# Products that nobody reads, put into TensorE's order of a two-layer transformer kernel

## The chip, the cores and the metric

One core of one Trainium2 chip runs the whole kernel. The metric is the device time of one execution in microseconds (us), the median of several runs; smaller is better.

## The reference, cut to what matters

The input is a batch of 8 sequences of 512 tokens by 256 features, in fp32. Four blocks follow one another, each wrapped the same way; what matters here is which matrix products there are.

```python
x = x + layernorm(attention0(layernorm(x)))   # 16 heads of 16, rope, causal softmax, biases
x = x + layernorm(gated_ffn0(layernorm(x)))   # silu(x Wg) * (x Wu), 768 wide, then Wd
x = x + layernorm(attention1(layernorm(x)))   # 16 heads of 64, 50*tanh(s/50), causal softmax
x = x + layernorm(token_shift_ffn(layernorm(x)))  # r = sigmoid(xr Wr); out = r * (relu(xk Wk)^2 Wv)
```

The attention of layer 0 has 16 heads of only 16 features; that of layer 1 has 16 heads of 64. Both mask with a lower triangle of 512 by 512.

## The kernel before, in words

**Precision.** Every weight and every activation that goes into a large product is split into a high and a low part (fp32r), and a product is three products: high by high, low by high, high by low (`split_terms`, L205; `product`, L336). The usual instruction on TensorE is therefore a product of 128 rows with 512 (or 256) columns.

**Two phases.** `phase1` (L356) does attention 0 and the gated ffn for all 8 batches, `phase2` (L1034) attention 1 and the token-shift ffn. The first writes its result to `x_mid` in DRAM, the second reads it.

**Pieces, rounds and the tables.** The work of a batch is cut into pieces ("rope", "max", "score", "pv", "o", "gate", ...). A table (L422 for layer 0, L1090 for layer 1) gives each piece a time. A round has 24 units of such time (`SLOTS`, L194). `Schedule` (L67) takes the quotient of a piece's time by 24 as the number of rounds by which it lags its batch, and the remainder as its place in the round. Every engine issues its own pieces in order of place; so the numbers only make an order for each engine, and semaphores do all the waiting. In one round of layer 0 TensorE works on the attention of batch b+1, on the ffn of batch b and on the projections of batch b+2. The middle rounds are a loop in the program; the first rounds and the last are written out. `start` (L499) merges the loading of weights (`loading_table`, L482) into the first round. `program` of phase 2 (L1190) merges layer 0's last rounds (`closing_table`, L1156), the loading of layer 1's weights (`prologue_table`, L1146) and layer 1's first rounds by `offset` (L1155).

**TensorE's pieces in layer 0.** "max" (`row_max`, L903) makes scores from 48 rows (L913) and adds a mask in bf16 (L920), for VectorE to take the row maxima (L782). "score" (L932) makes the scores again from 49 rows (L944), for ScalarE's exponential (L720). "pv" (L949) multiplies probabilities and values in four column strips of the array (L958). "outT", "att_T" and "x1_T" are transposes (L967, L978), "maxT" too (L928). "rope", "v", "o", "gate", "up" and "down" go through L340.

**The middle of a round.** After "o" of batch b VectorE has to form its statistics, its norm, the residual sum, the next statistics and the next norm (`o_out` to `x1_norm`, L811 to L837) before TensorE can transpose the result ("x1_T") and begin "gate". Meanwhile TensorE has only "max" and "score" of batch b+1, then "pv" of its first heads.

**Buffers in PSUM.** Rings of units (`Units`, L102) hold the results: `ring_d` for "max", "rope", "pv"; `ring_s` (two banks) for "score" and "v"; `ring_e` (banks 6 and 7) for "att_T", "o", "x1_T", "gate", "up", "down". `claim` (L162) makes TensorE wait until the unit's last user has been read. In phase 2 `ring_s` has two units of two banks for "v", "qk", "score", "x3_T", "r", "key" and "out".

**The end.** After the last attention piece "o" of batch 7 only "x3_T", "r", "key" and "out" are left for TensorE, and each waits for a chain over VectorE, ScalarE and GpSimd.

Of the kernel before, what the change touches and what calls it, by code (L numbers as in the profile page):

```python
# [27 lines left out]
P = 128  # L28
# [170 lines left out]
PLACED = 16 * 3 * 2  # L199
VSTEP = HD0 + 1  # L200
# [155 lines left out]
def phase1(nc, block, ctx, memory, a, x_mid, tok, banks, psum, ident, expo):  # L356
# [56 lines left out]
    with nc.sbuf_tensor("l0_staging", [P, 2 * NM, T], F32, side="right") as raw:  # L413
# [9 lines left out]
        "load_x": {(): -22.66},  # L423
        "x_stats": {(): -19.43},
        "x_rstd": {(): -21.11},
        "x_norm": {(): -18.09},
        "x_T": {(0,): -12.64, (1,): -12.6},
        "x_T_hi": {(0,): -13.41, (1,): -11.44},
        "x_T_lo": {(0,): -13.57, (1,): -13.43},
        "rope": {(0,): -6.98, (1,): -6.78, (2,): -0.17, (3,): 5.18},  # L430
# [1242 lines left out]
```

How the kernel before makes its waits and increments, by code:

```python
    def filled(self, eng, b, *use):  # L146
        eng.wait_ge(self.full, self.count(self.iteration(b, use), use, self.order))
# [1 line left out]
    def freed(self, eng, b, *use):  # L149
        eng.wait_ge(self.empty[self.freers[use]], self.count(self.iteration(b, use), use, self.group(use)))
# [11 lines left out]
    def claim(self, pe, b, *use, also=()):  # L162
        found = [user for user in (self.last_user(b, one) for one in (use, *also)) if user]
        for freer in self.empty:
            users = [user for user in found if self.freers[user[2]] == freer]
            if users:
                _, it, last = max(users, key=lambda user: user[0])
                pe.wait_ge(self.empty[freer], self.count(it, last, self.group(last)))
# [84 lines left out]
    def load(self, sp, n):  # L254
        if n >= self.slots:
            sp.wait_ge(self.low_done, n - self.slots + 1)
        sp.dma_start(self.raw(n), self.plan[n][0]).then_inc(self.loaded[n % self.slots], 16)
# [1 line left out]
    def high(self, act, n):  # L259
        act.wait_ge(self.loaded[n % self.slots], 16 * (n // self.slots + 1))
        self.nc.scalar.activation(self.plan[n][1], self.raw(n), ACT.Copy).then_inc(self.high_done, 1)
# [1 line left out]
    def low(self, dve, n):  # L263
        dve.wait_ge(self.high_done, n + 1)
        self.nc.vector.tensor_tensor(self.plan[n][2], self.raw(n), self.plan[n][1].bitcast(F32),
                                     ALU.subtract).then_inc(self.low_done, 1)
# [25 lines left out]
    def split(self, pe, i, count):  # L292
        if isinstance(i, int) and i == 0:
            pe.wait_ge(self.low_done, count)
```

## Time and profile before

| | |
|---|---|
| median of 3 runs | 1667.13 us (1666.17 to 1668.99) |
| profiled execution | 1666.39 us |
| its span, first to last instruction | 1664.6 us |
| TensorE busy | 1517.2 us, 91% of the span |
| VectorE, ScalarE, GpSimd busy | 1068.6, 833.4, 834.3 us |
| mean granted TensorE clock | 0.946 of 2.4 GHz |

The profile is of one execution. The span leaves out 1.8 us that lie around the first and the last instruction. In its views PE is TensorE, DVE VectorE, ACT ScalarE, POOL GpSimd, SP the queue that issues most DMAs. The granted clock is given as a share of 2.4 GHz: 1.00 is 2.4 GHz and 0.50 is 1.2 GHz; a value between them is a stretch that had both. "Busy" counts an engine as busy while an instruction of it is under way.

### The profile page before, as it was taken

How to read it: one execution, taken by the hardware profiler on the slowest of the kernel's cores; microseconds unless marked ns; L12 is line 12 of the kernel's file. 1: busy time of each engine (PE TensorE's matmuls, PEld its weight loads, DVE VectorE, ACT ScalarE, POOL GpSimd, SP SyncE). 2: the span in 40 equal slices, each digit the busy share in tenths (PEclk: the TensorE clock that was granted, in tenths of full speed). 3: DMA queues.
4: the chain of work that ended last, by engine and by line, in shares of the span. 5: the costliest groups of instructions: out<-in, count | busy, mean ns of one | idle time of the engine just before them, and what ended most of it. 6: DMA issues, size and time to landing. Idle time of an engine off the chain costs nothing.

```text
span 1664.6 us, 29499 instructions
## 1 busy us (share of the span) xinstructions
PE 1517.2 (91%) x11040; PEld 1090.6 (66%) x11040; DVE 1068.6 (64%) x1796; ACT 833.4 (50%) x1205; POOL 834.3 (50%) x1012
## 2 busy tenths in 40 slices
PE   3698999999998989898999999999999999999953
PEld 2455666757576766666767777777767677777742
DVE  4556676777767676666664667566675766666562
ACT  2233444443444435354465665756666566665621
POOL 2132433434344434343556666766658566585642
PEclk9677999999999999998999999999999999999986
DMA  6333333332323333321110001010000101000000
GB/s 145 68 52 52 52 64 52 52 56 36 61 37 61 42 63 40 64 90 39 45 39 1 1 5 35 1 39 1 27 10 0 38 0 38 0 1 26 1 26 13
DMA packets 46770, 61.34 MB, mean 37 GB/s; under 512 B 4928, under 2 KB 31968, under 8 KB 46688
## 3 DMA queue, kind: packets, MB, share of 16 engines
q1 hardware_dynamic: 45824, 59.56, 18.3%
q8 instruction: 55, 0.90, 0.2%
q10 hardware_dynamic: 864, 0.66, 0.1%
q14 instruction: 27, 0.22, 0.1%
HBM read 26.35 MB, written 8.39 MB: 21 GB/s over the span
## 4 chain that ended last, share of the span: by engine, by line
PE 83%; DVE 8%; ACT 3%; issue 2%; POOL 2%; DMA 2%; SPq 1%; POOLq 0%; DVEq 0%; ACTq 0%
PE psum L340 41%; PE psum L1588 8%; PE psum L1563 8%; PE psum L1604 5%; PE psum L958 5%; PE psum L1576 4%; PE psum L944 4%; PE psum L913 3%; DVE l_rowmax L782 2%; PE psum L920 1%; ACT l_probs L1369 1%; PE psum L978 1%; ACT l_probs L720 1%; PE psum L967 1%; PE psum L928 1%
## 5 line engine op out<-in xcount | busy, mean ns | idle before, releaser
L720 ACT ACTIVATE l_probs<-psum 128x512 f32<-128x512 f32 (+1 forms) x384 | 181.1, 524 | 243.9 <-PE psum L944 243.8
L1448 DVE RECIPROCAL l_att<-psum 128x512 f32<-128x512 f32 x64 | 214.8, 3356 | 96.5 <-PE psum L1576 86.3
L782 DVE TENSOR_REDUCE l_rowmax<-psum 128x2 f32<-128x1024 f32 (+3 forms) x256 | 200.8, 818 | 58.3 <-PE psum L920 57.6
L1369 ACT ACTIVATE l_probs<-psum 128x1024 f32<-128x1024 f32 (+1 forms) x192 | 163.8, 879 | 136.2 <-PE psum L1563 136.2
L221 POOL TENSOR_SCALAR_AFFINE_SELECT l_probs<-l_probs 128x256 f32<-128x256 f32 (+1 forms) x384 | 180.6, 502 | 0.0
L1439 DVE TENSOR_TENSOR l_qk_lo<-psum,l_qk_hi 128x1024 fp32r<-128x1024 f32 x64 | 77.9, 1218 | 143.2 <-ACT l_qk_hi L1359 143.2
L1375 ACT ACTIVATE l_probs<-l_probs 128x2048 f32<-128x2048 f32 (+1 forms) x128 | 160.1, 1270 | 1.3
L216 POOL TENSOR_TENSOR l_pool_holder<-expo 128x1 f32<-128x1 f32 x128 | 29.2, 228 | 243.3 <-ACT l_probs L720 121.8
L1588 PE MATMUL psum<-l_probs,l_v 128*64 128x512 f32 (+3 forms) x1024 | 150.7, 436 | 0.0
L1588 PEld LDWEIGHTS psum<-l_probs,l_v 128*64 128x64 f32 x1024 | 70.4, 137 | 83.3 <-issue 69.0
L1311 POOL TENSOR_TENSOR l_attT_lo<-l_att,l_attT_hi 128x512 fp32r<-128x512 f32 x64 | 93.7, 1469 | 61.4 <-ACT l_attT_hi L1387 61.2
L1303 POOL TENSOR_TENSOR l_keysum<-l_probs 128x768 f32<-128x768 f32 x64 | 118.2, 1846 | 6.9 <-POOL l_probs L221 0.4
L944 PE MATMUL psum<-l_qT,l_kT 49*128 49x512 f32 (+3 forms) x512 | 96.8, 415 | 25.7 <-ACT l_probs L720 23.5
L913 PE MATMUL psum<-l_kT,l_qT 48*128 48x512 f32 (+3 forms) x512 | 88.0, 384 | 27.7 <-DMA l_qT<-l_roped_hi 12.5
L667 POOL TENSOR_TENSOR l_hT_lo<-l_gated,l_hT_hi 128x512 fp32r<-128x512 f32 x48 | 61.8, 1287 | 90.0 <-ACT l_hT_hi L734 90.0
L650 POOL TENSOR_TENSOR l_roped_lo<-l_straight,l_turned 128x512 f32<-128x512 f32 x32 | 41.1, 1285 | 130.7 <-DVE l_turned L775 125.0
L1359 ACT ACTIVATE l_qk_hi<-psum 128x1024 fp32r<-128x1024 f32 x64 | 65.8, 1028 | 77.1 <-PE psum L340 77.1
L1563 PE MATMUL psum<-l_qk_hi 64*128 64x512 f32 (+3 forms) x512 | 96.9, 373 | 6.3 <-ACT l_probs L1369 2.8
L328 POOL TENSOR_TENSOR l_x_rstd<-l_x_veps,expo 128x4 f32<-128x4 f32 x48 | 50.8, 1058 | 98.4 <-DVE l_x_veps L322 97.8
L958 PE MATMUL psum<-l_probs,l_v 128*32 128x512 f32 (+3 forms) x1024 | 94.8, 521 | 0.0
L913 PEld LDWEIGHTS psum<-l_kT,l_qT 48*128 48x128 f32 x512 | 50.6, 207 | 54.2 <-issue 32.4
L1305 POOL TENSOR_TENSOR l_keysum<-l_keysum,l_probs 128x512 f32<-128x512 f32 x64 | 83.4, 1303 | 5.0
(196 smaller groups left out, 4173.9 us busy)
## 6 DMA issues: line engine op xcount, KB each, us to landing
l_kT<-l_roped_hi SPq DMA_DIRECT2D x64, 128.0 KB, 4.0
l_qT<-l_roped_hi SPq DMA_DIRECT2D x64, 128.0 KB, 5.8
l_xin<-in_x SPq DMA_DIRECT2D x8, 512.0 KB, 5.0
l_kT<-l_roped_lo SPq DMA_DIRECT2D x32, 128.0 KB, 5.1
l_qT<-l_roped_lo SPq DMA_DIRECT2D x32, 128.0 KB, 6.4
l_x<-in_x SPq DMA_DIRECT2D x8, 512.0 KB, 4.0
x_mid<-l_x SPq DMA_DIRECT2D x8, 512.0 KB, 4.6
l_xin<-x_mid SPq DMA_DIRECT2D x8, 512.0 KB, 4.4
```

What stands on the lines that cost most here:

```text
L221: nc.gpsimd.affine_select(out=part, in_=part, compare_op=ALU.is_ge, fill=0.0, base=0, pattern=[[0, part.shape[1]], [1, P]], channel_multip ...
L340: last = nc.tensor.matmul(out, l(c), r(c), start=(k == 0), stop=(k == len(todo) - 1))
L720: ring_s.free(nc.scalar.activation(probs[:, SLOT[p], e, c0:c1], ring_s.unit(*use)[:, 0:c1 - c0], ACT.Exp, scale=HD0 ** -0.5), *use)
L782: reduced = nc.vector.tensor_reduce(rowmax[:, t, a // 2, :, a % 2], ring_d.unit("max", a, k)[:, :, c0:c0 + (t + 1) * P], mybir.AxisListTyp ...
L913: nc.tensor.matmul(unit[:, e, c0:c0 + (t + 1) * P], qT[rows, a, t * P:(t + 1) * P], kT[rows, a, 0:(t + 1) * P], start=(c0 == 0), stop=False)
L944: last = nc.tensor.matmul(ring_s.unit("score", p, u, e)[:, c0:c0 + T - kt * P], kT[rows, p, kt * P:(kt + 1) * P], qT[rows, p, kt * P:T], s ...
L958: last = nc.tensor.matmul(ring_d.unit("pv", g)[32 * j:32 * j + 32, 0, kt * P:T], v0[:, kt, h * VSTEP:h * VSTEP + 32], probs[:, SLOT[p], j ...
L1369: ring_s.free(nc.scalar.activation(probs[:, p % 2, :, c0:c1], ring_s.unit("score", p, u)[:, :, 0:c1 - c0], ACT.Tanh, scale=HD1 ** -0.5 / C ...
L1375: nc.scalar.activation(part, part, ACT.Exp, scale=CLAMP).then_inc(exped.sem, 1)
L1448: ring_d.free(nc.vector.reciprocal(att[p % 2][:], ring_d.unit("den", p)), "den", p)
L1563: last = nc.tensor.matmul(ring_s.unit("score", p, u)[:, e, c0:c0 + T - kt * P], l[half, slot, 1, kt * P:(kt + 1) * P], r[half, slot, 0, kt ...
L1588: last = nc.tensor.matmul(ring_d.unit("pv", p)[64 * e:64 * e + 64, kt * P:T], v1[:, kt, 2 * p + e, :], probs[:, p % 2, e, OFF1[kt]:OFF1[kt ...
```

## The change

It adds matrix products whose results nobody reads. `heat` issues `count` products of 128 rows by 128 weights with 512 columns. They stand in three places:

- "warm": 16 pieces of 2 products in TensorE's order of layer 0's first round, into bank 7, which no piece uses in that round. They wait for nothing.
- "heat": 3 pieces of 2 products in each of layer 0's rounds for the 8 batches, at places 13.30, 14.90 and 15.28, that is after "o" and before "x1_T". They claim the unit of `ring_e` that "x1_T" will take. For batch 7 the closing table puts all three after layer 1's second "qk" piece.
- "end_heat": 9 pieces of 6 products, for batch 7 alone. They claim the unit of the piece that follows ("x3_T", "r" or "out"). In the last round the first stands after "o" of pair 3, the second after "o" of pair 5, the third between "o" of pair 7 and "x3_T"; three between "x3_T" and "r"; three between "key" and "out".

All other numbers of the tables change too, by amounts that swap neighbours in the engines' orders. No piece is added beside these, and none is removed.

```diff
+START_HEATS = 16
+ROUND_HEATS = 3
+END_HEATS = 9
...
+def heat(nc, out, w, count):
+
+    for _ in range(count):
+        nc.tensor.matmul(out, w[:, 0, 0:P], w[:, 0, 0:T], start=True, stop=True)
...
-        "score": {(0, 0): 9.1, (0, 1): 9.89, (0, 2): 11.93, (1, 0): 12.95, (1, 1): 14.48, (1, 2): 15.27, (2, 0): 15.31,
+        "score": {(0, 0): 8.67, (0, 1): 9.75, (0, 2): 12.12, (1, 0): 12.87, (1, 1): 14.74, (1, 2): 15.17, (2, 0): 15.37,
...
-        "x1_T": {(0,): 40.2, (1,): 40.82},
+        "x1_T": {(0,): 41.07, (1,): 41.07},
...
+        "heat": {(0,): 37.3, (1,): 38.9, (2,): 39.28},
...
+        "warm": {(0,): 1.4, (1,): 1.77, (2,): 2.92, (3,): 4.82, (4,): 5.99, (5,): 7.25, (6,): 7.8, (7,): 8.58, (8,): 9.46, (9,): 12.28, (10,): 12.35, (11,): 14.2, (12,): 15.5, (13,): 17.55, (14,): 18.78, (15,): 23.9},
...
+        def warm(n):
+
+            heat(nc, banks[7], wqk[0], 2)
+
+        def warm_round(i, n):
+
+            ring_e.claim(pe, i, "x1_T", 0)
+            heat(nc, ring_e.unit("x1_T", 0), wgu[0], 2)
...
+        "end_heat": {(0,): 26.17, (1,): 30.91, (2,): 38.43, (3,): 39.88, (4,): 41.31, (5,): 41.52, (6,): 42.61, (7,): 44.75, (8,): 44.97},
...
-    offset = 242.15
+    offset = 240.24
...
+        "heat": {(0, 7): 244.453, (1, 7): 244.505, (2, 7): 244.558},
...
+        def end_heat(i, n):
+
+            if isinstance(i, int) and i == BATCH - 1:
+                following = "x3_T" if n < 3 else "r" if n < 6 else "out"
+                ring_s.claim(pe, i, following)
+                heat(nc, ring_s.unit(following)[:, 0, :], wrkv[0], 6)
```

By the new tables TensorE's order in the middle of a layer-0 round becomes: "o" (second half), "score" (1,0), heat, "max" (4,0), "maxT", "score" (1,1), heat, "max" (4,1) and (4,2), "score" (1,2), heat, "score" (2,0), "max" (5,0), "pv" (0), "score" (2,1), "max" (5,1), "rope" (0), "x1_T". Before, "x1_T" (0) stood right behind "pv" (0), ahead of "score" (2,1), "max" (5,1) and "rope" (0), and its second half ahead of that "rope".

## Rows read from the trace of the kernel before

**Rows 1.** The page: busy time of the engines, and the chain that ended last.
```profile
PE 1517.2 (91%) x11040; PEld 1090.6 (66%) x11040; DVE 1068.6 (64%) x1796; ACT 833.4 (50%) x1205; POOL 834.3 (50%) x1012
...
PE 83%; DVE 8%; ACT 3%; issue 2%; POOL 2%; DMA 2%; SPq 1%; POOLq 0%; DVEq 0%; ACTq 0%
```

**Rows 2.** The page: granted clock in 40 slices of the span, in tenths.
```profile
PEclk9677999999999999998999999999999999999986
```

**Rows 3.** Windows, TensorE alone: stretch, length, busy us (instructions), granted clock, DMA.
```profile
45.00:127.00 82.00, 67.90 (x462) 0.67 0.33 55
136.00:144.00 8.00, 7.13 (x56) 0.57 0.26 51
157.00:168.00 11.00, 8.98 (x68) 0.53 0.01 1
249.00:257.00 8.00, 6.28 (x47) 0.57 0.01 3
...
693.00:701.00 8.00, 6.86 (x54) 0.57 0.01 2
754.00:766.00 12.00, 8.73 (x31) 0.57 0.44 131
```

**Rows 4.** Windows, TensorE alone: the long stretches of both layers, and the end.
```profile
180.00:740.00 560.00, 526.62 (x4272) 0.96 0.33 55
800.00:1590.00 790.00, 783.24 (x5408) 1.00 0.05 16
1590.00:1664.00 74.00, 28.98 (x165) 0.69 0.07 22
```

**Rows 5.** Timeline of TensorE, middle of a layer-0 round: start, us, line, gap before and its releaser.
```profile
426.13 0.38 PE L944 MATMUL psum<-l_qT,l_kT 49*128 49x256 f32 x2 [1.17 <-ACT l_probs L720]
427.26 0.80 PE L944 MATMUL psum<-l_qT,l_kT 49*128 49x512 f32 x2 [0.74 <-ACT l_probs L720]
...
429.28 0.79 PE L913 MATMUL psum<-l_kT,l_qT 48*128 48x512 f32 x2 [0.83 <-DVE l_rowmax L782]
...
430.19 4.16 PE L958 MATMUL psum<-l_probs,l_v 128*32 128x512 f32 x32
434.32 0.66 PE L978 MATMUL psum<-ident,l_gated 128*128 128x128 f32 x4
```

**Rows 6.** Windows, TensorE alone, around the same place of that round.
```profile
413.00:416.00 3.00, 2.64 (x24) 1.00 0.84 126
...
424.00:427.00 3.00, 1.21 (x18) 1.00 0.48 169
427.00:430.00 3.00, 1.92 (x12) 0.51 0.00 0
```

**Rows 7.** Timeline of TensorE: products at both levels of the clock.
```profile
749.25 2.36 PE L958 MATMUL psum<-l_probs,l_v 128*32 128x512 f32 x32
...
762.01 0.63 PE L340 MATMUL psum<-l_xT_hi,l_wq_lo 128*128 128x512 f32 x1
762.44 0.63 PE L340 MATMUL psum<-l_xT_hi,l_wq_hi 128*128 128x512 f32 x1
...
1639.08 0.39 PE L340 MATMUL psum<-l_mixk_hi,l_wrkv_hi 128*128 128x512 f32 x1
1639.31 0.39 PE L340 MATMUL psum<-l_mixk_lo,l_wrkv_hi 128*128 128x512 f32 x1
```

**Rows 8.** Windows, TensorE alone: the end of the kernel.
```profile
1604.00:1608.00 4.00, 0.56 (x5) 1.00 0.39 131
1608.00:1611.00 3.00, 2.55 (x12) 0.51 0.44 139
...
1624.00:1634.00 10.00, 0.00 (x0) 0.50 0.00 0
1634.00:1639.00 5.00, 4.96 (x24) 0.52 0.00 0
...
1642.00:1648.00 6.00, 0.03 (x1) 0.80 0.00 0
1648.00:1653.00 5.00, 5.00 (x24) 0.56 0.00 0
```

More of the change, by code:

```diff
@@ new lines, in phase1 @@
+        "x_T_hi": {(0,): -13.01, (1,): -11.01},
+        "x_T_lo": {(0,): -13.31, (1,): -12.99},
+        "rope": {(0,): -7.32, (1,): -6.78, (2,): -1.09, (3,): 5.18},
+        "roped": {(0,): -8.61, (1,): -5.33, (2,): 0.74, (3,): 4.84},
+        "rope_sum": {(0,): -10.57, (1,): -8.49, (2,): 2.44, (3,): 3.85},
+        "rope_hi": {(0,): -4.41, (1,): -3.91, (2,): 6.25, (3,): 6.5},
+        "rope_lo": {(0,): -6.33, (1,): -3.74, (2,): 6.23, (3,): 7.06},
+        "place": {(0,): -1.66, (1,): -1.47, (2,): 8.29, (3,): 8.95},
@@ new lines, in phase1 @@
+        "outT_norm": {(0,): 19.3, (1,): 26.21, (2,): 29.66, (3,): 31.89},
+        "att_T": {(0,): 34.01, (1,): 34.47},
+        "att_T_hi": {(0,): 34.59, (1,): 34.72},
+        "att_T_lo": {(0,): 33.16, (1,): 34.17},
+        "o": {(0,): 35.64, (1,): 36.15},
+        "o_out": {(0,): 34.45, (1,): 35.85},
+        "x1_T": {(0,): 41.07, (1,): 41.07},
+        "x1_T_hi": {(0,): 40.99, (1,): 41.13},
+        "x1_T_lo": {(0,): 39.99, (1,): 40.94},
+        "o_stats": {(): 36.13},
+        "o_rstd": {(): 34.77},
@@ new lines, in phase1 @@
+        "hidden": {(0,): 44.69, (1,): 48.09, (2,): 49.93, (3,): 51.31, (4,): 52.39, (5,): 53.02},
+        "hidden_hi": {(0,): 45.77, (1,): 47.6, (2,): 50.21, (3,): 50.43, (4,): 53.71, (5,): 54.94},
+        "hidden_lo": {(0,): 43.71, (1,): 45.49, (2,): 45.93, (3,): 50.21, (4,): 51.99, (5,): 51.99},
+        "down": {(0,): 55.87, (1,): 56.16, (2,): 56.2, (3,): 56.69},
+        "heat": {(0,): 37.3, (1,): 38.9, (2,): 39.28},
+        "x2_stats": {(): 55.56},
+        "x2_rstd": {(): 57.81},
+        "x2_norm": {(): 56.21},
@@ new lines, in phase2 @@
+        "x3_T_out": {(): 37.36},
+        "mix": {(0,): 39.34, (1,): 41.51},
+        "mix_hi": {(0,): 37.7, (1,): 40.28},
+        "mix_lo": {(0,): 38.18, (1,): 38.82},
+        "r": {(): 41.72},
+        "r_out": {(): 41.76},
+        "key": {(): 42.25},
+        "key_out": {(): 42.2},
+        "square": {(): 42.09},
+        "kact_hi": {(): 43.99},
+        "kact_lo": {(): 46.6},
+        "out": {(): 45.41},
+        "out_out": {(): 47.32},
+        "gate": {(): 47.36},
+        "x4_stats": {(): 47.9},
@@ new lines, in phase2 @@
+        "att_T": {(0, 7): 239.67, (1, 7): 241.68},
+        "o": {(0, 7): 243.927, (1, 7): 244.163},
+        "heat": {(0, 7): 244.453, (1, 7): 244.505, (2, 7): 244.558},
+        "x1_T": {(0, 7): 245.73, (1, 7): 245.94},
+        "gate": {(0, 7): 246.66, (1, 7): 247.28, (2, 7): 248.997, (3, 7): 249.06, (4, 7): 249.32, (5, 7): 250.287},
+        "up": {(0, 7): 246.83, (1, 7): 247.56, (2, 7): 249.003, (3, 7): 249.11, (4, 7): 249.48, (5, 7): 250.383},
+        "down": {(0, 7): 251.912, (1, 7): 252.094, (2, 7): 252.276, (3, 7): 252.458},
@@ L1631, in key @@
             ring_s.fill(last, "key")
[L1633 removed]
+        program(pe, {"end_heat": end_heat, "x_T": x_T, "v": v, "qk": projected, "score": score, "den": den, "pv": pv, "o": o,
                      "x3_T": x3_T, "key": key, "r": tokens("r", mixr, slice(0, D), mix_split, 2 * NC),
```

242 lines of the change are left out of this document (98 added, 144 removed).

## The prediction, made before the changed kernel ran

> **What bounds the kernel now.** I read the page first. TensorE is busy for 91% of the span and makes 83% of the chain that ended last [rows 1]. Its clock comes next, as it decides what a busy microsecond is worth: full nearly everywhere, but low at the start, at the end, and dented between them [rows 2]. The windows place the dents [rows 3]. In the first round TensorE is busy for 67.9 of 82 us at a mean clock of 0.67; then come a dip at 136, one in the middle of each of seven rounds (at 157, 249, 338, 427, 515, 604 and 693 us; the first, second and last are shown) and one where the layers meet, at 754. Layer 1 has none: 783.2 of 790 us busy at 1.00, so it can hardly gain [rows 4]. The end is the opposite: 29.0 us busy of 74, at 0.69.
>
> What a stretch would give at full clock I take as its busy time times what the clock lacks of 1.00 (work done in B us at a mean clock c fills B times c at full clock). It overrates where another engine's chain sets the pace, as the gaps stay. The sum: first round 67.9 x 0.33 = 22.4 us; dip at 136, 3.1; at 157, 4.2; six others between 2.7 and 3.0, together 17; at 754, 3.8; the end 29.0 x 0.31 = 9.0, of which 2.0 would only widen gaps, so 7. In all 57 us, 3.4% of the time: the most that a full clock could bring before its price.
>
> Why does it fall? In the round at 427 no gap is long: 1.17, 0.74 and 0.83 us, behind ScalarE's exponentials and VectorE's maxima [rows 5]. But from 424 to 427 TensorE was busy for only 1.21 of 3 us, with products of 48 and 49 rows, and the clock fell right after; where it was busy for 2.64 of 3 it stayed full [rows 6]. It came back only behind the "pv" group, which took 4.16 us there and 2.36 us at full clock [rows 5, 7].
>
> A page of the Trainium skill reads differently: "TensorE: Matmul & The Clock Gate", section "Why this matters for your kernels", asks for no long idle gaps between bursts and says nothing against many short ones. By it these dips should not be there; the trace disagrees, with 1.17 us the longest gap in front of the fall. What that would mean for the change is a rival below.
>
> **The change, part by part.** A product costs 0.23 us at full clock and 0.43 us at the low one, the distance of two starts [rows 7]. Its result goes to PSUM units that are free, so apart from TensorE's time it costs only its `claim`. No DMA is added, and SP's order swaps only weight fetches and one "maxima" with neighbours that wait for other things; I cost that at nothing, hidden behind TensorE.
>
> *First round, 32 products.* The first pair stands behind the first "max", whose DMA ends at about 45 us, so the clock is already low when it comes; nothing stands in the idle stretch ahead. I take 60% of the 22.4 us as regained, 13.4: the first pairs need some us to lift the clock, and two products every 3 to 5 us will not hold it each time. Bounds: 0% and 100%. Price: 32 x 0.23 = 7.4 us, and some 10 of them at the low level add 2.0. TensorE is idle for 14.1 us here; with 2.7 us of the products in such gaps, 6.7 stay on the path. Net 6.7 faster; bounds 13.7 slower (none regained, all 32 at 0.43 on the path) and 20 faster.
>
> *Layer-0 rounds, 6 products each.* The three pieces stand behind "score" (1,0), (1,1) and (1,2), where TensorE next waits for ScalarE: gaps of about 0.7, 1.17 and 0.74 us against 0.46 us a pair. So they cost nothing while those gaps last; without the cover, 6 x 0.23 = 1.4 us a round. The `claim` waits for VectorE's read of "o", done before. Seven rounds hold 4.2 + 17 = 21 us. I take three quarters, 15.9 us: the gap of 0.83 at 428 has no product in it, and "pv" could still meet a low clock. What is late next is VectorE's norm: "x1_T" waits for it at 434.3, and a "pv" faster by 1.8 us would meet that wait. The new order puts "rope" (12 to 24 products, 2.8 to 5.5 us) ahead of "x1_T", which covers it. Bounds: 21 faster; 7 x 1.4 = 9.8 slower.
>
> *Batch 7's six.* They come behind "qk", after the gaps that lower the clock at 754, so they don't lift it; two transposes for layer 1 move ahead of "att_T", into such a gap. Net 0.5 faster; bounds 1.4 slower, 3.8 faster.
>
> *The end, 54 products.* "x3_T" stays low: only 6 products precede it in more than 10 us of idleness. Between "x3_T" and "r" 18 run for 4.1 to 7.7 us of the 10 idle ones; "r" took 4.96 us at 0.52 and would take 2.7 [rows 8]. I count 1.3 of those 2.2, since some idle time is left before "r". Behind "key" 18 at full clock fill 4.1 of 6 us, and "out" (5.00 us at 0.56, so 2.2 to gain) gets 1.8. The 6 in front of "o" of pairs 6 and 7 lie in the gap at 1604 and give 0.6 of 1.2. Sum 3.7 faster; bounds 2 slower (a group late by its own length delays what is queued behind it), 6.3 faster. All of them finish, by the lengths above, before their follower is ready.
>
> *The other places.* They swap neighbours. Layer 1 has 6.8 us of idle time in all, so they can't gain there, and could lose; the retuned order of layer 0 could give or take a few us. I take 0, bounds 8 either way.
>
> Sum: 6.7 + 15.9 + 0.5 + 3.7 = 26.8 faster. Against the profiled execution, 1666.4 - 26.8 = 1639.6; that execution lies 0.7 us below the median shown, so I say 1640.
>
> **The rivals.**
>
> *Nearly all the clock comes back.* The places look fitted to the gaps, and the first round's pairs are spread over all of it. Then about 52 of 57 us return, less 9 of price: 1667 - 43 = 1624. Against it: the dip at 754 has no products ahead of it, and "x3_T" stays low. 0.15.
>
> *The rounds' dips stay.* Six short products do not outweigh 48-row work and gaps; or, as that page has it, only long gaps matter, and what fills short ones does nothing. Then the 15.9 are gone, and the first round nets about 3: 1667 - 7 = 1660. For it: between 427 and 430 TensorE was busy for 1.92 of 3 us even at half speed [rows 6]. Against it: 0.92 us of full-height products in a stretch busy for 1.21 of 3 is a large addition. 0.14.
>
> *The new order gives part of it back.* Layer 1 runs at 99% busy; 1.5 us lost in each of its 8 rounds make 12: 1652. 0.10.
>
> *Slower: the products queue in front of work that is ready.* TensorE takes them in order. If the clock stays low in the first round, 32 x 0.43 = 13.7, less 4 in gaps, are 10 us lost; in the rounds half of 8 x 6 x 0.23 lies on the path, 5.5; at the end 1: 1667 + 16 = 1683. It decides once less than a third of the first round's 22 us and none of the dips come back. 0.07.
>
> The same page, in its section on what happens when a matmul is issued, says that products stay in program order while only weight loads are pulled ahead. That is the rule against this change; no row here shows a product overtaking another, and by its figure for 512 columns back to back (about 0.22 us) the 32 would cost 6.9 us instead of 7.4.
>
> That the products are dropped is no case: they are plain instructions, and 134 of them (32 + 48 + 54) will be there.
>
> **How the numbers follow.** The forecast has 0.54, its own range 1630 to 1652; the rivals as given. The range holds all of the first, most of the second, the order's case and the nearer part of the dips' case: 1622 to 1660. Below it lies 0.07, above it 0.13. A measurement of this kernel can tell about 0.2% (3.3 us) from no change. Faster by more than that: 0.88. Within it: 0.04. Slower: 0.08.
>
> **What would show it.** First round: the mean clock of its window at 0.8 or more, and its length down by 5 to 9 us although 32 products are added. Rounds: no value below 1.00 around "pv" (0) in at least five of seven, "pv" at 2.4 us, the round 2 to 3 us shorter. End: "r" and "out" together down from 10 to about 7 us. Layer 1: the loop's rounds equal to within 0.5 us. I am wrong if the clock still falls in front of "pv" (0) in most rounds, if the mean clock of the first round stays under 0.75, or if ScalarE's or VectorE's waits in front of "score" and "max" grow by what the clock gave.

## The result: 1.2% slower, and the profile after

| | before | after |
|---|---|---|
| median of the runs made side by side | 1667.44 us (1666.17 to 1668.99, 4 runs) | 1689.32 us (1682.62 to 1689.98, 4 runs) |
| span of the profiled execution | 1664.6 us | 1687.1 us |
| mean granted TensorE clock | 0.946 | 0.965 |

The ratio is 1.0122, 95% interval [1.0095, 1.0149]. The forecast was 1640 us, and its range ended at 1660: wrong by sign. The clock rose as meant, and the time rose too.

The page of the changed kernel: busy time, granted clock in 40 slices, shares of the chain that ended last. It answers to [rows 1, 2].

```profile
PE 1540.6 (91%) x11174; PEld 1110.6 (66%) x11174; DVE 1085.9 (64%) x1796; ACT 825.3 (49%) x1205; POOL 823.2 (49%) x1012
...
PEclk9789999999999999999999999999999999999997
...
PE 75%; DVE 7%; issue 5%; ACT 5%; POOL 3%; DMA 3%; SPq 2%; POOLq 0%; ACTq 0%; DVEq 0%
```

TensorE held 83% of the chain before and holds 75% now; ScalarE, POOL, DMA, SP's queue and "issue" have gained shares. So other engines end more waits. The waits of TensorE name one (line, releaser: us in all, times, longest):

```profile
PE psum L924 <- DMA l_qT<-l_roped_hi: 26.8, 6, 14.6
```

Before, this wait came once, with the 12.5 us of the first round. Now it comes five times more, 12.2 us together: "max" waits for the load of the q rows. Windows of TensorE in the changed kernel (stretch, length, busy us, clock, DMA share, GB/s), against [rows 3, 4, 8]:

```profile
45.00:127.00 82.00, 66.59 (x474) 0.79 0.40 59
...
153.00:242.00 89.00, 83.14 (x688) 1.00 0.34 50
...
331.00:423.00 92.00, 85.93 (x688) 0.96 0.31 52
...
474.00:478.00 4.00, 4.00 (x18) 0.57 0.20 69
...
1657.00:1661.00 4.00, 4.00 (x19) 0.50 0.00 0
```

The first stretch's clock went from 0.67 to 0.79. Two rounds (from 153 and from 242) have no dip at all. From 331 on the old dip is back, and a second one stands 50 us into the round (474 to 478), behind the new wait. "r" at the end (1657) is as slow as before. Both are in the timeline of the round that begins at 423.6, "pv" (0) and "max" (0,0):

```profile
436.61 4.05 PE L969 MATMUL psum<-l_probs,l_v 128*32 128x512 f32 x32 [0.18 <-DVE l_rowmax L793]
...
473.96 0.50 PE L924 MATMUL psum<-l_kT,l_qT 48*128 48x512 f32 x2 [1.92 <-DMA l_qT<-l_roped_hi]
```

To say where time went I cut each trace where "x_T" starts: at the third round, at the last round of layer 0's loop, at layer 1's second round, at its last. Lengths in us of all kernels of this study, from their profiled executions:

| kernel | to the third round | layer-0 rounds | join of the layers | layer-1 rounds | end |
|---|---|---|---|---|---|
| before | 149.7 | 444.6 | 269.7 | 612.7 | 187.9 |
| after | 153.1 | 454.6 | 274.3 | 613.7 | 191.4 |
| tables_only | 154.7 | 462.6 | 272.5 | 613.6 | 191.0 |
| products_only | 151.0 | 451.1 | 269.0 | 612.7 | 186.2 |
| pool_order | 152.3 | 454.3 | 273.1 | 613.7 | 190.9 |
| pool_swap_alone | 146.3 | 485.1 | 284.8 | 612.8 | 189.2 |
| rope_chain | 148.3 | 438.3 | 268.7 | 613.7 | 190.9 |
| rope_pool | 149.4 | 438.2 | 270.0 | 613.8 | 192.4 |
| old_layer0 | 150.9 | 449.9 | 268.5 | 613.7 | 191.4 |
| mask_alone | 148.7 | 455.1 | 273.8 | 613.7 | 192.4 |
| mask_early | 152.3 | 470.3 | 274.8 | 612.5 | 187.9 |
| repaired_bare | 147.6 | 443.3 | 272.6 | 613.7 | 191.3 |
| round_only | 149.9 | 445.6 | 269.0 | 612.7 | 187.9 |
| end_only | 144.9 | 447.7 | 269.0 | 612.5 | 184.2 |
| warm_only | 151.8 | 447.5 | 272.4 | 612.7 | 188.7 |
| warm_early | 148.9 | 447.6 | 272.5 | 612.6 | 188.8 |
| round_double | 149.5 | 448.7 | 270.2 | 612.7 | 186.8 |
| chain_double | 151.3 | 434.4 | 270.7 | 613.7 | 191.3 |
| x1_behind | 150.2 | 460.3 | 274.6 | 612.7 | 187.8 |
| x1_behind_end | 148.8 | 463.2 | 276.3 | 612.7 | 186.6 |

The 22.5 us of the change are 3.4 + 10.0 + 4.6 + 1.0 + 3.5. A row is one execution: that of `rope_chain` was its fastest (1661.6 us, median 1666.0), the others lie nearer to their medians.

### The profile page after: what moved, and what is told of

Same layout as the page of the kernel before. It is cut to its first block, busy times and chain, and to the rows that moved or that the text cites. A ratio compares the mean times of both kernels' runs of the same rounds, so it can differ in the third digit from the quotient of the medians.

```text
span 1687.1 us, 29762 instructions
## 1 busy us (share of the span) xinstructions
PE 1540.6 (91%) x11174; PEld 1110.6 (66%) x11174; DVE 1085.9 (64%) x1796; ACT 825.3 (49%) x1205; POOL 823.2 (49%) x1012
## 4 chain that ended last, share of the span: by engine, by line
PE 75%; DVE 7%; issue 5%; ACT 5%; POOL 3%; DMA 3%; SPq 2%; POOLq 0%; ACTq 0%; DVEq 0%
PE psum L343 37%; PE psum L1611 8%; PE psum L1586 7%; PE psum L1627 5%; PE psum L969 4%; PE psum L1599 4%; PE psum L955 3%; PE psum L924 3%; ACT l_probs L1392 2%; DMA l_qT<-l_roped_hi 2%; DVE l_rowmax L793 2%; SPq L603 1%; ACT l_probs L731 1%; PE psum L931 1%; PE psum L989 1%
## 5 line engine op out<-in xcount | busy, mean ns | idle before, releaser
L224 POOL TENSOR_SCALAR_AFFINE_SELECT l_probs<-l_probs 128x256 f32<-128x256 f32 (+1 forms) x384 | 174.3, 486 | 0.0
L924 PE MATMUL psum<-l_kT,l_qT 48*128 48x512 f32 (+3 forms) x512 | 84.6, 368 | 45.0 <-DMA l_qT<-l_roped_hi 26.8
L1334 POOL TENSOR_TENSOR l_attT_lo<-l_att,l_attT_hi 128x512 fp32r<-128x512 f32 x64 | 85.8, 1340 | 36.8 <-ACT l_attT_hi L1410 36.7
L924 PEld LDWEIGHTS psum<-l_kT,l_qT 48*128 48x128 f32 x512 | 48.0, 196 | 74.0 <-issue 39.2
L661 POOL TENSOR_TENSOR l_roped_lo<-l_straight,l_turned 128x512 f32<-128x512 f32 x32 | 41.2, 1287 | 96.0 <-DVE l_turned L786 88.5
L969 PE MATMUL psum<-l_probs,l_v 128*32 128x512 f32 (+3 forms) x1024 | 86.0, 482 | 2.0 <-POOL l_probs L224 1.2
```

The source lines that it names most:

```text
L224: nc.gpsimd.affine_select(out=part, in_=part, compare_op=ALU.is_ge, fill=0.0, base=0, pattern=[[0, part.shape[1]], [1, P]], channel_multip ...
L924: nc.tensor.matmul(unit[:, e, c0:c0 + (t + 1) * P], qT[rows, a, t * P:(t + 1) * P], kT[rows, a, 0:(t + 1) * P], start=(c0 == 0), stop=False)
L969: last = nc.tensor.matmul(ring_d.unit("pv", g)[32 * j:32 * j + 32, 0, kt * P:T], v0[:, kt, h * VSTEP:h * VSTEP + 32], probs[:, SLOT[p], j ...
```

## The experiments

**1. Order or products?** `tables_only` is the changed kernel without its 134 products, `products_only` the kernel before with them. `pool_order` takes one swap on POOL back in the changed kernel. `pool_swap_alone` moves one place in the kernel before; by its number "hidden_lo" (0) passes not only "rope_lo" (1) but "mask" (3) too, which it does not pass in the changed kernel.

```diff
 tables_only, against after: the lines "warm", "heat", "heat" (closing) and "end_heat" removed
 products_only, against before: these lines added; "end_heat": {(0,): 28.7, (1,): 30.91, (2,): 37.0,
   (3,): 38.5, (4,): 40.0, (5,): 41.0, (6,): 42.61, (7,): 44.0, (8,): 44.9}, "heat" of batch 7 at 246.2 to 246.4
 pool_order, against after
-        "rope_lo": {..., (1,): -3.74, ...
+        "rope_lo": {..., (1,): -4.5, ...
 pool_swap_alone, against before
-        "hidden_lo": {(0,): 44.58, ...
+        "hidden_lo": {(0,): 42.9, ...
```

> The changed kernel without any of its 134 extra products; all other new places stay. Theory O (the new order costs, the products are about neutral): about 1680 us, at least 1675. Theory P (the products queue in front of ready work, the order is neutral): 1663 to 1670 us, like the kernel before.

> The kernel before with the same three kinds of extra products (32 + 48 + 54), at the same places in TensorE's order as far as the old order has them (the nine at the end stand at the end's gaps, the first of them behind the last score of pair 7). Theory O: 1655 to 1668 us, no slower than before. Theory P: 1680 us or more.

> The changed kernel with one swap undone on GpSimd: the low part of the second rope piece goes ahead of the low part of the first hidden piece again, in every layer-0 round. If that swap makes TensorE wait 1.9 us for the placed rows of q in front of the first max and lets the clock fall a second time in a round (worth 1.7 us), as the trace of after suggests, about 3.5 us come back in each of 5 or 6 rounds: 1668 to 1674 us. If the swap is not the cause (theory P, or another swap): 1686 us or more.

> The kernel before with that one swap made on GpSimd and nothing else. If it is a cause by itself: 8 to 20 us slower than before (1675 to 1687), with a wait for the rows of q in each round. If it needs the other new places: within 3 us of before.

Measured, against before: `tables_only` 1695.3 us, 1.0170 [1.0153, 1.0187]; `products_only` 1671.6 us, 1.0033 [1.0021, 1.0045]; `pool_order` 1687.4 us, 1.0126 [1.0109, 1.0143]; `pool_swap_alone` 1719.5 us, 1.0312 [1.0295, 1.0329].

The other places alone cost more than the whole change. The products alone cost 5 us on before's places and give 6 on the new ones (1695.3 to 1689.3). Both runs on POOL missed what was expected of them. The single swap back gave 2 us instead of 15 to 20. One number moved on POOL cost 52 us instead of 8 to 20, and by another wait than the changed kernel has, in TensorE's "pv" for POOL's masks:

```profile
PE psum L958 <- POOL l_probs L221: 36.0, 7, 5.4
```

The wait for the q rows stayed there as it was before (13.2 us in all, before 12.5), and in the changed kernel "pv" waits for a mask once, for 1.2 us. So POOL's order matters, but `pool_swap_alone` is no copy of the changed kernel's fault. POOL in a steady round of the kernel before (start, us, line, operation, gap before and its releaser); L650 forms a rotary sum, L654 its low part ("rope_lo"), L221 masks:

```profile
440.86 1.29 POOL L650 TENSOR_TENSOR l_roped_lo<-l_straight,l_turned 128x512 f32<-128x512 f32 x1 [8.01 <-DVE l_turned L775]
...
444.97 1.28 POOL L654 TENSOR_TENSOR l_roped_lo<-l_roped_lo,l_roped_hi 128x512 fp32r<-128x512 f32 x1 [1.36 <-ACT l_roped_hi L698]
446.21 1.29 POOL L650 TENSOR_TENSOR l_roped_lo<-l_straight,l_turned 128x512 f32<-128x512 f32 x1
450.13 1.28 POOL L654 TENSOR_TENSOR l_roped_lo<-l_roped_lo,l_roped_hi 128x512 fp32r<-128x512 f32 x1 [2.63 <-ACT l_roped_hi L698]
```

And the same in the changed kernel, whose lines are L661, L665 and L224:

```profile
446.17 1.29 POOL L661 TENSOR_TENSOR l_roped_lo<-l_straight,l_turned 128x512 f32<-128x512 f32 x1 [6.76 <-DVE l_turned L786]
...
450.30 1.28 POOL L661 TENSOR_TENSOR l_roped_lo<-l_straight,l_turned 128x512 f32<-128x512 f32 x1 [1.39 <-DVE l_turned L786]
456.03 0.19 POOL L219 TENSOR_TENSOR l_pool_holder<-expo 128x1 f32<-128x1 f32 x1 [4.45 <-ACT l_probs L731]
456.17 1.36 POOL L224 TENSOR_SCALAR_AFFINE_SELECT l_probs<-l_probs 128x512 f32<-128x512 f32 x3
457.49 1.29 POOL L665 TENSOR_TENSOR l_roped_lo<-l_roped_lo,l_roped_hi 128x512 fp32r<-128x512 f32 x1
```

Before, the first low part comes 4.1 us after its sum. After, "mask" (3) stands between (place 16.89 instead of 20.52, with "rope_lo" (0) at 17.67): POOL waits 4.45 us for ScalarE's exponential, and the low part comes 11.3 us after its sum. Behind it hang the copies of the k rows ("place" (0), after "rope_lo" (0)) and of the q rows ("place" (1), after "rope_lo" (1)), and behind these "max" (0,0).

**2. Repairs of the changed tables.** `rope_pool` moves two places on POOL, `mask_alone` only the second of them, `rope_chain` one on ScalarE as well; `old_layer0` takes layer 0's places from before.

```diff
 rope_pool, against after (mask_alone: the "mask" line alone)
-        "rope_lo": {..., (1,): -3.74, ...
+        "rope_lo": {..., (1,): -4.5, ...
-        "mask": {..., (3,): 16.89, ...
+        "mask": {..., (3,): 19.6, ...
 rope_chain: this, and
-        "rope_hi": {(0,): -4.41, ...
+        "rope_hi": {(0,): -5.9, ...
 old_layer0: layer 0's table and the loading table of before, with the lines "warm" and "heat"
```

> As rope_chain, but only the two places on POOL are moved (rope_lo 1 and mask 3); ACT keeps the changed kernel's order, rope_hi (0) behind maxT_out (2) and tanh (0). It tells POOL's part from ACT's. If POOL's mask (3), which waits 4.45 us for exp (3,2) in front of rope_lo, is the whole cause: equal to rope_chain within 3 us. If ACT's rope_hi is late by itself: within 3 us of the changed kernel (1684 to 1690), and only rope_chain is faster. Theory P: no effect, 1684 to 1690.

> The changed kernel (1689 us) with three places of layer 0's table moved, so that the rotary pieces of the next batch come first on their engines: rope_lo (1) and mask (3) on POOL (order rope_lo 0, rope_lo 1, mask 3, hidden_lo 0), and rope_hi (0) on ACT from -4.41 to -5.9, ahead of exp (3,1) and maxT_out (2). The 134 products and all else stay. Theory O (the tables' other places cost the time, through the late placing of q and k rows: max (0,0) waits for the l_qT load, TensorE idles and its clock falls a second time): the wait of L924 for l_qT shrinks from 26.8 us to under 14, the second dip of the steady rounds goes, a steady round takes 88.5 to 90 us instead of 92.0, the total 1667 to 1676. Theory P (products queued in front of ready work cost the time; the load's wait is a by-product): 1684 to 1690. Theory R (one place repaired only passes the wait on to the next one, as with rope_lo alone, which gave 2 us): the l_qT wait shrinks but max or rowmax waits grow as much, 1680 to 1688.

> The changed kernel with one place moved: layer 0's mask (3) on POOL from 16.89 to 19.6, behind rope_lo (0) and ahead of hidden_lo (0); rope_lo (1) stays at -3.74, behind hidden_lo (0). rope_lo (1) alone gave 2 us (1687.4), both together 24 us (1665.3). If mask (3) in front of rope_lo (0) is the whole cause (POOL waits 4.45 us for exp (3,2) there): 1665 to 1670. If the two only work together (rope_lo (1) behind hidden_lo (0) is late by itself, and either one delays the q rows): 1680 to 1688. If each takes its share: 1670 to 1680.

> The changed kernel with layer 0's table and the loading table as before, plus the 32 + 18 + 30 products of the first round and the rounds; layer 1's table, the prologue, offset and closing tables and the 54 end products stay those of the change. It splits the cost of the new places by layer. If the cost sits in layer 0's steady rounds (3.5 us in each of six) and layer 1 costs 0.65 us in each of seven rounds, 2 at the join and 3 to 5 at the end: 1677 to 1682. If layer 0 holds all of it: 1670 to 1674 (as the products on the old places, 1671.6). If layer 1 and the join hold most: 1684 or more.

Measured: `rope_pool` 1665.3 us, 0.9997 [0.9985, 1.0009]; `rope_chain` 1666.0 us, 0.9992 [0.9977, 1.0008]; `mask_alone` 1690.0 us, 1.0138 [1.0105, 1.0170]; `old_layer0` 1677.0 us, 1.0064 [1.0040, 1.0087].

Two numbers of the tables, both of POOL's pieces, take 24 us away by the medians, 21 by the two ratios (1.0122 and 0.9997). ScalarE's place adds nothing. TensorE's wait in `rope_pool`:

```profile
PE psum L924 <- DMA l_qT<-l_roped_hi: 15.9, 2, 14.6
```

Each number alone gives nothing (`pool_order` 2 us, `mask_alone` none). In `mask_alone` the mask is out of the way, but "rope_lo" (1) still stands behind "hidden_lo" (0) of the gated ffn, which waits for ScalarE in its turn:

```profile
451.03 1.27 POOL L665 TENSOR_TENSOR l_roped_lo<-l_roped_lo,l_roped_hi 128x512 fp32r<-128x512 f32 x1 [3.30 <-ACT l_roped_hi L709]
...
458.87 1.28 POOL L678 TENSOR_TENSOR l_hT_lo<-l_gated,l_hT_hi 128x512 fp32r<-128x512 f32 x1 [5.11 <-ACT l_hT_hi L745]
```

"max" needs the rows of both. SP's queue shows why each fault alone is enough. The copies it issues for "place" (0), k, and "place" (1), q, in `after`, in `pool_order` and in `rope_pool`:

```profile
458.86 2.55 SPq L603 DMA_DIRECT2D l_kT<-l_roped_hi  x4
465.27 1.18 SPq L603 DMA_DIRECT2D l_qT<-l_roped_hi  x2
```

```profile
457.71 2.56 SPq L603 DMA_DIRECT2D l_kT<-l_roped_hi  x4
461.68 1.19 SPq L603 DMA_DIRECT2D l_qT<-l_roped_hi  x2
```

```profile
444.83 2.56 SPq L603 DMA_DIRECT2D l_kT<-l_roped_hi  x4
448.81 1.18 SPq L603 DMA_DIRECT2D l_qT<-l_roped_hi  x2
```

The rounds begin at 423.6, 422.5 and 412.3 us. In these traces the twelve copies of a round land about 1.06 us apart. With only "rope_lo" (1) mended the q copies are issued 2.5 us earlier (39.2 us into the round, not 41.7), but they queue behind the k copies, which still start at 35.2, and the last lands at 50.1 us (50.2 in the changed kernel). In `mask_alone` the k copies start at 32.5, but the q copies only at 41.6, and the last lands at 50.0. With both mended it lands at 47.4 (before: 46.8), and "max" no longer waits. So two faults that each hold the same piece look like none when only one is mended. In `old_layer0` layer 1's rounds and end are as long as in the changed kernel (613.7 and 191.4 us, before 612.7 and 187.9), so layer 1's new places cost about 4.5 us. Which of them do was not tried.

**3. The mirror.** `mask_early` moves the mask alone in the kernel before. There it passes not only both "rope_lo" but also the second sum, "rope_sum" (1), which stays ahead of it in the changed kernel.

```diff
-        "mask": {(0,): 12.65, (1,): 13.31, (2,): 15.86, (3,): 20.52, ...
+        "mask": {(0,): 12.65, (1,): 13.31, (2,): 15.86, (3,): 15.865, ...
```

> The mirror: the kernel before, without any product, with one place moved, mask (3) on POOL from 20.52 to 15.865, ahead of rope_lo (0). If that order costs what the tables cost: a steady round of 91 to 92.5 us instead of 88.6, a new wait of L923's line for the l_qT load, a second clock dip beside the first, and a total of 1682 to 1696. If it is the combination with the change's other places that costs (in the tables of before rope_hi (0) stands earlier on ACT, so that rope_lo has slack): 1666 to 1672.

Measured: 1697.95 us, 1.0182 [1.0161, 1.0203]; a steady round takes 94.2 us. Both are above what was expected (1682 to 1696, 91 to 92.5), and the path is another one. Its POOL:

```profile
465.96 0.19 POOL L216 TENSOR_TENSOR l_pool_holder<-expo 128x1 f32<-128x1 f32 x1 [6.02 <-ACT l_probs L720]
466.10 1.35 POOL L221 TENSOR_SCALAR_AFFINE_SELECT l_probs<-l_probs 128x512 f32<-128x512 f32 x3
467.42 1.29 POOL L654 TENSOR_TENSOR l_roped_lo<-l_roped_lo,l_roped_hi 128x512 fp32r<-128x512 f32 x1
468.67 1.26 POOL L650 TENSOR_TENSOR l_roped_lo<-l_straight,l_turned 128x512 f32<-128x512 f32 x1
```

and two of its waits, of ScalarE and of TensorE:

```profile
ACT l_roped_hi L698 <- POOL l_roped_lo L650: 44.0, 10, 8.5
...
PE psum L944 <- ACT l_probs L720: 43.6, 32, 4.0
```

Here the second sum is late too (468.67), ScalarE stands 44.0 us in all in front of its "rope_hi" (15.3 before) with exponentials queued behind, and TensorE waits 43.6 us for these (23.5 before) instead of for the load. So a mask too early costs here too, but this is not the changed kernel's path; that one is shown by the repairs, where only the two numbers differ.

The Trainium skill, "PSUM — Partial Sum Buffer", section "Engine vs sequencer instructions", calls the queues of ScalarE, VectorE and GpSimd strictly first in, first out. The trace agrees: in the changed kernel ScalarE had finished the high parts by 455.3 us, and yet POOL began the low part at 457.49, behind the mask for which it had sat idle for 4.45 us.

**4. The products without the fault.** `repaired_bare` is `rope_chain` without any of the 134 products.

> rope_chain (1666.0 us) without its 134 products: the changed tables with the rotary pieces in front. It gives what the products are worth on an order that does not wait for l_qT. On the tables of before they cost 4.8 us (1671.6 against 1666.8), on those of the change they gave 6 (1689.3 against 1695.3). If they only fill a hole that the late rows made: 1658 to 1664. If they hold the clock whatever the order: 1669 to 1675. In the steady rounds I expect 2.9 us of clock lost instead of 1.7 or none, against 2.2 us of work less: 88 us a round, no change.

Measured: 1671.8 us, 1.0034 [1.0023, 1.0046]. So the products give about 6 us on the repaired order (1666.0 against 1671.8). The total is that of the second case, in which they hold the clock whatever the order. It is not so everywhere: they gain in layer 0 (the loop's rounds 443.3 to 438.3 us, the join 272.6 to 268.7 by the fastest execution, 270.0 by that of `rope_pool`), nothing at the end, and on before's places they cost.

**5. One kind of product at a time,** on before's places: `round_only` (48), `end_only` (54), `warm_only` (32).

> The kernel before with the 48 products of layer 0's rounds alone (six a round in front of pv 0); no start or end products, no other place moved. My prediction gave 15.9 us for this. From products_only (a steady round 88.6 us with and without them: 1.3 us of clock and 1.0 us of gaps filled against 2.2 us of added work) it should be neutral: 1664 to 1669. If the products in front of the late dip really were worth three quarters of the 21 us and the start products ate it: 1648 to 1656. If they only queue in front: 1672 to 1678.

> The kernel before with the 54 end products alone (places 28.7 to 44.9 of layer 1, last batch). My prediction gave 3.7 us for them; products_only's end stretch was 1.6 us shorter than before's. If the forecast's mechanism holds at that size: 1664 to 1666, r and out at 2.7 to 4 us instead of 5.0. If they only queue: 1667 to 1669.

> The kernel before with the 32 start products alone, at the change's places 1.4 to 23.9 of the first round. My prediction gave 6.7 us net for them. Of the 4.8 us that all products cost on the tables of before (1671.6), the rounds' own cost 3.3 (1670.1) and the end's gave 5 (1661.6), so that about 5 to 7 are left for the start products: 1669 to 1674, with the first x_T of batch 2 at 151 us instead of 149.7 and the next at 245 instead of 239.6. If the prediction's mechanism held: 1658 to 1662.

Measured: `round_only` 1670.1 us, 1.0018 [1.0004, 1.0032]; `end_only` 1661.6 us, 0.9970 [0.9953, 0.9986]; `warm_only` 1677.2 us, 1.0066 [1.0054, 1.0079]. Their sum is 9 us slower (3.0 - 5.0 + 11.0), all three together 5.5. Each lies outside what was expected of it: `round_only` by 1 us and `warm_only` by 3 on the slow side, `end_only` by 2 on the fast side.

The end pays: 5.0 us (2.3 to 7.8 by the interval), 3.7 were forecast. TensorE in `end_only` (the 18 products, and the start of "r" and of "out"):

```profile
1621.06 6.63 PE L350 MATMUL psum<-l_wrkv_hi 128*128 128x512 f32 x18 [1.11 <-ACT l_xs L1420]
1630.38 0.36 PE L343 MATMUL psum<-l_wrkv_hi,l_mixr_hi 128*128 128x256 f32 x1 [2.69 <-POOL l_mixk_lo L1336]
...
1636.07 4.27 PE L350 MATMUL psum<-l_wrkv_hi 128*128 128x512 f32 x18
1642.21 0.36 PE L343 MATMUL psum<-l_wrkv_hi,l_kact_hi 128*128 128x256 f32 x1 [1.88 <-POOL l_kact_lo L1341]
```

"r" runs at full clock here (a window from 1630.3 to 1633.1 shows 1.00; before, 0.52 [rows 8]), "out" only at its start. The end stretch is 3.7 us shorter, as large as the sum's term. Another execution shows less: with the same products in the same places "r" takes 4.5 us in `products_only` and 4.6 in `x1_behind_end`, not the 3.0 of this one, and their end stretches are 1.7 and 1.3 us shorter than before's; that of `round_double`, which has no product there, is 1.1 shorter.

**6. The first round: place or price?** `warm_early` puts all 16 pairs ahead of "max" (0,0), into the 12.5 us of its wait.

```diff
+        "warm": {(0,): 0.05, (1,): 0.095, ... (15,): 0.725},   (in steps of 0.045)
```

> As warm_only, but all 16 pairs stand ahead of max (0,0) (places 0.05 to 0.73), in the 12.5 us in which TensorE waits for the first l_qT load (32.5 to 45.0 us). 32 products take 7.4 us at full clock and 13.8 at the low one, so they fit or nearly. If the place is what was wrong (the clock is low when the first pair comes): the clock is full from 45 us on for at least a few us, the first batch is 2 to 5 us shorter, 1662 to 1666. If the sparse work behind it lets the clock fall again whatever stands ahead: no gain, 1665 to 1669, and the window 45 to 82 us at the same mean clock as before (0.67) within 0.07. If they delay the loads or the first max: 1670 or more.

Measured: 1672.8 us, 1.0039 [1.0026, 1.0051]. Timeline and windows of TensorE:

```profile
32.02 7.42 PE L350 MATMUL psum<-l_wqk_hi 128*128 128x512 f32 x32
44.69 0.80 PE L923 MATMUL psum<-l_kT,l_qT 48*128 48x512 f32 x2 [5.25 <-issue]
```

```profile
32.00:45.00 13.00, 7.75 (x35) 0.96 1.09 138
45.00:52.00 7.00, 5.80 (x46) 0.50 0.11 33
45.00:82.00 37.00, 26.70 (x180) 0.64 0.39 60
```

The 32 run at full clock and delay nothing ("max" starts at 44.69 us; 44.99 before). But 5.25 us of idle time follow, and the window from 45 to 52 us stands at 0.50, that from 45 to 82 at 0.64, as before. The case of "no gain whatever stands ahead" holds for this stretch (72.5 us against 73.0); the total was above it, by 4 us, for time lost further on (below, at the first round's step).

**7. Twice as many products.** `round_double` is `round_only` with 12 products a round, `chain_double` is `rope_chain` with 12.

```diff
-            heat(nc, ring_e.unit("x1_T", 0), wgu[0], 2)
+            heat(nc, ring_e.unit("x1_T", 0), wgu[0], 4)
```

> round_only (1670.1 us) with twice as many products: four for each heat piece, so 12 a round, 96 in all. Tells whether the rounds' term fails for want of products or by their price. Price in full: 48 x 0.23 = 11 us more, less what falls into gaps. If six were too few to hold the clock and twelve hold it: the dip in front of pv (0) goes (1.6 us a round) for 1.4 us of price, 1669 to 1673. If the dip does not come from those gaps alone: 1676 to 1682, a steady round 90 us instead of 88.6.

> rope_chain (1666.0 us: the changed kernel with its rotary pieces in front) with four products for each heat piece, 12 a round. There two kinds of steady rounds stand: 88.3 us with a dip worth 1.7 in front of pv (0), and 87.0 us without. If twelve hold the clock in every round and the added work lies in TensorE's wait for VectorE's maximum (1.45 us idle at 12.2 us of the round): rounds of 87.0 us, 1658 to 1663. If the added work lies on the path: 1668 to 1674.

Measured: `round_double` 1671.1 us, 1.0033 [1.0016, 1.0050]; `chain_double` 1662.7 us, 0.9974 [0.9965, 0.9984]. What a steady round of layer 0 is made of (the clock's loss is busy time times what the clock lacks of 1.00, summed over windows of half a microsecond; work is busy time less that loss):

| kernel, products a round | length | idle | loss | work |
|---|---|---|---|---|
| before, 0 | 88.6 | 4.9 | 2.9 | 80.8 |
| round_only, 6 | 88.6 | 4.0 | 1.6 | 83.0 |
| round_double, 12, from 421 | 88.6 | 4.3 | 0.0 | 84.3 |
| repaired_bare, 0 | 88.8 | 6.0 | 2.5 | 80.3 |
| rope_chain, 6, most rounds | 88.3 | 4.1 | 1.7 | 82.5 |
| rope_chain, 6, round at 411 | 87.0 | 4.1 | 0.0 | 82.9 |
| chain_double, 12, all | 87.0 | 2.8 | 0.0 | 84.2 |
| tables_only, 0 | 92.2 | 7.8 | 4.2 | 80.3 |
| after, 6, from 331 | 92.0 | 6.0 | 3.4 | 82.6 |

Twelve hold the clock in every steady round on the repaired order, and in the last two (from 421 and 510) on before's places. There it changes nothing: 88.6 us three times. The timelines tell why. `round_only` and `round_double`, "pv" (0) and then "x1_T":

```profile
431.55 3.54 PE L968 MATMUL psum<-l_probs,l_v 128*32 128x512 f32 x32
435.68 0.66 PE L988 MATMUL psum<-ident,l_gated 128*128 128x128 f32 x4 [0.58 <-DVE l_gated L335]
```

```profile
434.11 2.36 PE L968 MATMUL psum<-l_probs,l_v 128*32 128x512 f32 x32 [0.18 <-DVE l_rowmax L792]
438.37 0.66 PE L988 MATMUL psum<-ident,l_gated 128*128 128x128 f32 x4 [1.90 <-DVE l_gated L335]
```

From the start of their rounds (417.0 before, 418.3, 421.0) "x1_T" begins at 17.3, 17.4 and 17.4 us. "pv" got faster by 1.8 us (4.16 in [rows 5], 2.36 here), and the wait for VectorE's norm grew to 1.90 us. In the changed order "rope" (0) stands between "pv" and "x1_T", and no such wait is left. `chain_double`:

```profile
424.06 0.50 PE L924 MATMUL psum<-l_kT,l_qT 48*128 48x512 f32 x2 [0.23 <-DVE l_rowmax L793]
424.84 2.36 PE L969 MATMUL psum<-l_probs,l_v 128*32 128x512 f32 x32 [0.18 <-DVE l_rowmax L793]
431.22 0.82 PE L989 MATMUL psum<-ident,l_gated 128*128 128x128 f32 x6
```

Here the gain reaches the round: 87.0 us. The six further products filled what was a wait of 1.45 us for VectorE's maxima in `rope_chain`, and cost nothing.

**8. Taking that wait away on before's places.** `x1_behind` is `round_only` with "x1_T" behind "rope" (0); `x1_behind_end` adds the end products and has 12 a round.

```diff
-        "x1_T": {(0,): 40.2, (1,): 40.82},
+        "x1_T": {(0,): 41.07, (1,): 41.1},
```

> round_only (1670.1 us: the kernel before with the 48 round products) with x1_T moved behind rope (0) in TensorE's order (40.2 and 40.82 to 41.07 and 41.1), as in the changed table. In all three of before, round_only and round_double x1_T starts 17.4 us after the round's x_T, held by VectorE's norm (idle 0.4, 0.9, 2.3 us), and a steady round takes 88.6 us whatever the clock does; in the changed tables rope (0) stands between and covers that wait. If that wait eats what the clock gives: a steady round 86.5 to 87.9 us, 1658 to 1665. If something else holds the round at 88.6: 1666 to 1672.

> The version meant to beat both: the kernel before with x1_T behind rope (0), 12 products a round (96) and the 54 end products, no start products. If x1_behind gains (3 to 8 us under round_only), the twelve hold the clock in all rounds, and the end gives its 4 to 5: 1652 to 1660. If the rounds stay at 88.6: 1661 to 1668.

Measured: 1687.4 us, 1.0120 [1.0105, 1.0135], and 1687.0 us, 1.0114 [1.0099, 1.0129]. Both missed. The wait in front of "x1_T" is gone, but "x1_T" begins at 21.8 us of the round, and TensorE then waits for ScalarE and VectorE (1.23 us in front of "score", 0.56 in front of "rope"); a steady round takes 92 us. What ScalarE and VectorE have queued for "x1_T" stayed in its old place ahead of exponentials and maxima. I read it so; that these are what waits was not tested by moving them.

## Why the prediction was wrong, point by point

**"The other places. They swap neighbours ... I take 0, bounds 8 either way."** This step failed, and it is the largest single miss: they cost 28 us by themselves, against 0. It does not turn the sign alone, as the products' terms, 26.8 us together, failed too: on before's places all products cost 5 us, on the repaired ones the total is that of before. The step read TensorE's and SP's orders and gave POOL's none: "mask" (3), which passed both low parts and not one neighbour, ahead of "rope_lo" (0), and "hidden_lo" (0) ahead of "rope_lo" (1). Either puts a wait for ScalarE in front of what the next round's first "max" needs, and either alone lets the last q row land at 50 us of the round instead of 47. Shown by `rope_pool` (21 to 24 us back), with `pool_order` and `mask_alone` beside it, which differ from it by one number each. `mask_early` and `pool_swap_alone` (30 and 52 us) show only that such a move on POOL is dear; both pass a further piece and cost by other waits. Layer 1's places cost about 4.5 us, inside the bound. The rest of layer 0's new order is worth a little: `repaired_bare` has 443.3 us of rounds against 444.6.

**"I take three quarters, 15.9 us."** Mis-sized, with a right mechanism behind it. On before's places 48 products cost 3 us. The step counted "pv" as time of the path; it named the wait that is late next ("x1_T waits for it at 434.3") and took the new order as its cover. That was so: on before's places the wait eats everything, on the repaired new ones six give 0.5 us in most rounds and 1.8 where the dip stays away, twelve 1.8 in all (88.8 to 87.0). Three quarters of 2.9 us would have been 2.2. Six products hold the clock only in some rounds ("pv" took 4.05 us at 436.6 in the changed kernel, not the 2.4 that the text asked for). The sign "I am wrong if the clock still falls in front of "pv" (0) in most rounds" came true: it fell there in the four rounds from 331 on. "So they cost nothing while those gaps last" is wrong too: 2.2 us more work a round, of which 1.0 in gaps. By the spacing of starts six are 1.4 us; where the other 0.8 come from is open.

**"First round ... net 6.7 faster."** The clock came nearly as forecast (0.79 from 45 to 127 us; the text asked for 0.8, and called itself wrong under 0.75; the new places alone have 0.71, the products alone 0.81), the time did not. By `warm_only` these products make the kernel 11 us slower. Its first two rounds are 2.1 us longer, and there the terms can be read: from 45 us to the third round the clock's loss goes from 26.5 to 18.2 us (8.3 regained, 13.4 forecast), the work from 61.1 to 72.6 (11.5 of price, where 32 x 0.23 is 7.4), the idle time from 17.2 to 16.0 (1.2 of cover, 2.7 forecast). Another 2.9 lie in the rounds behind, 2.7 at the join and 0.8 at the end, where the kernel has no added product; the four make 8.5 of span. `warm_early`, whose products all end before 40 us, has 3.0, 2.8 and 0.9 in the same three, so these 6.4 do not hang on where the products stand. At the join the clock's loss differs: 6.1 us against 2.9 from 757 to 864. Such dips at the join and in the second round come and go between kernels that are the same there, by 2 to 5 us. I take them for the same gaps meeting the clock at other moments; no run isolates it.

**"The end ... 3.7 faster."** Right in size on before's places (3.7 us in `end_only`, but 1.7 and 1.3 in two others), wrong for the changed kernel. There the new places of layer 1 cost 3.4 us without any product, and with them the products gained nothing (191.4 with, 191.0 without; on the repaired order 190.9 and 191.3). "r" and "out" took 5.5 and 4.4 us, not the 7 together that the text asked for (5.2 and 5.1 before).

**Batch 7's six** were not tried alone.

**The rivals.** "The new order gives part of it back" was the right kind, placed in the wrong layer: layer 1's last five rounds of the cut lost 0.6 us each, not 1.5 (its first one gained 2.2), while layer 0's lost 3.4. "The rounds' dips stay" saw the clock of these four rounds rightly and put the time at 1660. "Products queue in front" ended near the measured time (1683) by luck, for a reason that was not this kernel's: without products it is slower still. The spans of four traces give the whole: +3.8 from before to `repaired_bare` (the places without POOL's fault, layer 1's 4.5 among them), -4.6 from there to `rope_pool` (the products, and one place of ScalarE that gave nothing), +23.3 from there to the changed kernel (the fault): 22.5.

**The page's rule.** The prediction weighed the section "Why this matters for your kernels" of the Trainium skill's page "TensorE: Matmul & The Clock Gate", which asks for no long idle gaps. Here the clock fell behind gaps of at most 1.17 us, and twelve products put into gaps under 1.5 us took the loss of a round from 2.9 us to none (2.5 to none on the repaired order). Another section of the same page of the Trainium skill, "A second HAM failure mode: psum-queue depth-cycling", does describe brief idleness between groups that lets the clock swing; the trace of the kernel before agrees with that one: gaps of 1.17 and 0.74 us stood where the clock fell to 0.51 [rows 5, 6].

## What to carry to other kernels

Before costing a retuned order at nothing, list for every engine, the least busy too, what now stands ahead of whom, and follow each waiting instruction to what is queued behind it: GpSimd is busy for half of this kernel, and two swaps on it cost 21 to 24 us. Filling gaps to hold the clock pays where TensorE's own work sets the next deadline; where the next piece waits for another engine at a fixed time, read that wait first. And when one repair brings nothing, mend the second suspect together with it before dropping either.

Two versions beat both kernels by little: `end_only` at 1661.6 us and `chain_double` at 1662.7.

## What the runs showed that I had not expected

- 32 products held the full clock for 7.42 us, and after 5.25 us of idleness the next instructions ran at half: in this run the full clock did not last across that wait.
- A mask too early in one queue shows as a wait for a DMA in one order and as a wait for ScalarE's exponentials in another. A trial that moves one number can pass two pieces: count what it passes before taking it for a copy of the fault.
- A change in the first 80 us moves dips 600 us later by 2 to 3 us. Between two traces a difference of that size in one stretch is no finding.
